# An attention and feed-forward layer: the attention result goes channel-major through DRAM instead of through transposes, orders are new, tiles are laid at multiples of 256 bytes

## What is computed

```python
def attn(x, w_qkv, b_qkv, w_out, b_out):          # 16 heads of 16 channels
    q, k, v = split(x @ w_qkv.T + b_qkv)
    scores = einsum('bhqd,bhkd->bhqk', q * hd ** -0.5, k) + mask
    out = einsum('bhqk,bhkd->bhqd', softmax(scores), v)
    return out.transpose(0, 2, 1, 3).reshape(B, L, D) @ w_out.T + b_out

def ffn(h, W1, b1, W2, b2):                       # 256 -> 1024 -> 256
    return relu(h @ W1 + b1) @ W2 + b2

x = x + layernorm(attn(layernorm(x), ...))
x = x + layernorm(ffn(layernorm(x), ...))
```

## Time and profile before

| | us |
|---|---|
| median of three runs (2044.54 to 2048.37) | 2048.34 |
| the profiled execution, its own time | 2041.29 |
| its span in the trace | 2039.5 |

### The profile page before, as it was taken

One profiled execution on the slowest core, in us unless ns is written; L12 is line 12 of the kernel. 1 busy time (PEld: TensorE's weight loads), 2 busy tenths in 40 slices (PEclk: granted clock), 3 DMA queues, 4 the chain that ended last, 5 costly groups with the idle time before them and its releaser, 6 DMA issues. The chain is left out here.

```text
span 2039.5 us, 71012 instructions
## 1 busy us (share of the span) xinstructions
PE 1926.4 (94%) x27904; PEld 1575.7 (77%) x27904; DVE 1511.4 (74%) x2913; ACT 1406.0 (69%) x2343; POOL 741.6 (36%) x910
## 2 busy tenths in 40 slices
PE   5789999999999999999999999999999999999985
PEld 3458888777878877888777788787788887778775
DVE  4687777787777778778777777777777777876731
ACT  1457767777776777776677777677777677776763
POOL 3113333334333334433343433333433333343343
PEclk7799999999999999999999999999999999999997
DMA  5333434433333433333343333343334344333200
GB/s 144 74 70 80 89 77 86 85 76 82 81 81 79 93 79 80 79 81 81 82 85 80 79 77 81 80 94 78 77 77 86 76 87 85 78 81 69 56 28 17
DMA packets 132815, 160.60 MB, mean 79 GB/s; under 512 B 29408, under 2 KB 82400, under 8 KB 132576
## 3 DMA queue, kind: packets, MB, share of 16 engines
q1 hardware_dynamic: 130544, 154.13, 35.7%
q10 hardware_dynamic: 2032, 2.69, 0.4%
HBM read 38.21 MB, written 17.83 MB: 27 GB/s over the span
## 5 line engine op out<-in xcount | busy, mean ns | idle before, releaser
L817 DVE TENSOR_REDUCE max_bias<-p_pair 128x4 f32<-128x1024 f32 (+1 forms) x640 | 772.8, 1222 | 262.0 <-PE p_pair L571 139.8
L742 ACT ACTIVATE probs<-p_pair 128x1024 f32<-128x1024 f32 x640 | 634.8, 1026 | 208.4 <-PE p_pair L568 127.6
L964 POOL TENSOR_TENSOR h_lo<-h_f,h_hi 128x512 fp32r<-128x512 f32 x256 | 329.7, 1288 | 507.5 <-ACT h_hi L774 507.5
L571 PE MATMUL p_pair<-stack 49*128 49x256 f32 (+1 forms) x3072 | 319.6, 306 | 39.5 <-DVE max_bias L817 22.7
L774 ACT ACTIVATE h_f<-p_pair,b_s 128x256 f32<-128x256 f32 x512 | 248.8, 486 | 133.1 <-PE p_pair L598 133.1
L571 PEld LDWEIGHTS p_pair<-stack 49*128 49x128 f32 (+1 forms) x3072 | 226.9, 188 | 126.7 <-DVE max_bias L817 59.8
L598 PE MATMUL p_pair<-w_hi,h_hi 64*128 64x256 f32 x2048 | 309.4, 279 | 5.0 <-ACT h_hi L774 2.5
L598 PE MATMUL p_pair<-x_hi,w_hi 64*128 64x256 f32 (+1 forms) x2560 | 302.1, 306 | 9.6 <-DVE x_lo L827 5.2
L598 PE MATMUL p_pair<-w_hi,h_lo 64*128 64x256 f32 x2048 | 305.7, 275 | 0.0
L598 PE MATMUL p_pair<-w_lo,h_hi 64*128 64x256 f32 x2048 | 305.5, 275 | 0.0
L598 PE MATMUL p_pair<-x_hi,w_lo 64*128 64x256 f32 (+1 forms) x2560 | 297.7, 302 | 0.0
(11 more groups left out here) (81 smaller groups left out, 2792.9 us busy)
## 6 DMA issues: line engine op xcount, KB each, us to landing
stack<-qk SPq DMA_DIRECT2D x1536, 64.0 KB, 2.3
xr<-x SPq DMA_DIRECT2D x32, 512.0 KB, 4.2
out<-yf SPq DMA_DIRECT2D x64, 256.0 KB, 2.2
xa<-x SPq DMA_DIRECT2D x31, 512.0 KB, 3.8
shift_rows<-max_t SPq DMA_DIRECT2D x128, 8.0 KB, 1.4
stack<-shift_rows SPq DMA_DIRECT2D x128, 8.0 KB
probs<-w_qkv_t SPq DMA_DIRECT2D x2, 384.0 KB, 5.5
ya<-w ACTq DMA_DIRECT2D x1, 512.0 KB, 8.2
```

The lines of the kernel that those rows point to most:

```text
L571: last = nc.tensor.matmul(dst[:, j, col:col + HALF].rearrange("p (a n) -> p a n", a=2), stack[r, stationary, at, kb * P:(kb + 1) * P], two ...
L742: nc.scalar.activation(probs[:, prob_slot(quad, c), :, :], banks("scores", n)[:, :, :], ACT.Exp, scale=SCALE).then_inc(exp_done, 1)
L817: nc.vector.tensor_reduce(dst, src, axis=AX.X, op=ALU.max, negate=True).then_inc(red_done, 1)
L964: nc.gpsimd.tensor_tensor(h_parts[1][:, m:m + 2, :], h_f[:, n % 2, :, :], h_parts[0][:, m:m + 2, :].bitcast(F32), ALU.subtract).then_inc(h ...
```

## The change

The four `o_t` and the one `o2` of PE are gone, and with them five fills of a PSUM pair a batch. In their place the result stays channel-major and goes through DRAM:

- `store_o` (SP, 4 a batch) sends the 128x512 result of one `pv` to `o_rows` (256 KB), and its four rows of sums to `den_q` in SBUF (8 KB), spread over the partitions.
- `inverse` (DVE, 2 a batch) takes the reciprocals of 128x32 sums, `store_inv` sends them to `inv_rows` in DRAM, and `load_inv` brings them back, each row to 16 partitions (`inv_b`, 256 KB written a time).
- `load_o` (SP, 2 a batch) brings the 16 channels of 8 heads into `o_ch`, which is the memory of `ya` (256 KB); `normal_o` (DVE, 2 a batch) multiplies `o_ch` by `inv_b`; `o2_hi` and `o2_lo` split it in two halves of 128x512 each, SBUF to SBUF.
- Channels now come in the order channel of the head, then head; the rows of w_out are put in that order on the host side of the inputs. `o_t` has two buffers.

All five engines have new lists. The small and odd tiles stand behind the large ones, and `max_bias` is padded, so that every matmul operand begins at a multiple of 256 bytes from `w_hi`, but the slices of `values`.

```diff
 ORDER = {
     "PE": [
-        ("scores_max", 16, -2, 2), ("qk", 1, -1, 3), ("scores", 6, -2, 0), ("pv", 0, -2, 1),
+        ("f1", 7, -4, 3), ("qk", 2, -1, 1), ("scores_max", 1, -1, 0), ("max_t", 3, -2, 2), ("qk", 3, -1, 1),
...
-        bqk_s, b1_s = sb("bqk_s", [P, 4]), sb("b1_s", [P, KF])
         b2_s = sb("b2_s", [P, D])
-        minus_half, eps = sb("minus_half", [P, KB]), sb("eps", [P, KB])
         xa = sb("xa", [P, KB, D])
...
-        max_bias = sb("max_bias", [P, 2, 4 * KB + D])
-        o_t = sb("o_t", [P, L])
-        den = sb("den", [P, 2, 2 * KB])
-        o_n = sb("o_n", [P, KB, D])
+        o_t = sb("o_t", [P, 2, L])
+        inv_b = sb("inv_b", [P, KD, L])
+        o_rows = nc.dram_tensor("o_rows", [KD, H // 2, 32, L], F32, kind="Internal").ap()
+        inv_rows = nc.dram_tensor("inv_rows", [KD, H // 2, L], F32, kind="Internal").ap()
         ya = sb("ya", [P, KB, D])
+        o_ch = ya[:, :, :].rearrange("p (c a) n -> p c (a n)", c=KD)
...
+        max_bias = sb("max_bias", [P, 2, 5 * P // 2])
+        den_q, inv_q = sb("den_q", [P, KD, 2, DT]), sb("inv_q", [P, KD, 2, DT])
...
+                elif what == "store_o":
+                    wait(sp, ot_done, b, QUADS, n + 1)
+                    reached(sp, o_in[n // 2], rows_free)
+                    reached(sp, inv_done, den_free)
+                    sp.dma_start(den_q[:, n // 2, n % 2, :],
+                                 o_t[HD:P:32, n % 2, :].rearrange("h (m t) -> h m t", t=DT)).then_inc(den_in[n % 2], 16)
+                    sp.dma_start(o_rows[n // 2, heads].rearrange("h c n -> (h c) n"),
+                                 o_t[:, n % 2, :]).then_inc(o_out[n % 2], 16)
+                elif what == "load_o":
+                    wait(sp, o_out[0], b, 32, 16 * (n + 1))
+                    reached(sp, o_out[1], other)
+                    reached(sp, x1_done, added)
+                    sp.dma_start(o_ch[:, n, :], o_rows[n, :, 0:HD, :].rearrange("h c n -> c h n")).then_inc(o_in[n], 16)
+                elif what == "store_inv":
+                    wait(sp, inv_done, b, KD, n + 1)
+                    sp.dma_start(inv_rows[n].rearrange("(j h) (m t) -> (h m) j t", j=2, t=DT),
+                                 inv_q[:, n, :, :]).then_inc(inv_out[n], 16)
+                elif what == "load_inv":
+                    wait(sp, inv_out[n], b, 16, 16)
+                    reached(sp, on_done, read)
+                    sp.dma_start(inv_b[:, n, :],
+                                 inv_rows[n].unsqueeze(0).broadcast_to([HD, H // 2, L])).then_inc(inv_in[n], 16)
...
-                elif what == "o2":
-                    wait(pe, ev["o_t"], b, QUADS, QUADS)
-                    last = transposed(dst, lambda r, m: o_n[r, m % KB, m // KB * P:(m // KB + 1) * P], KD * KB)
-                elif what == "o_t":
-                    wait(pe, ot_done, b, QUADS, n + 1)
-                    last = transposed(dst, lambda r, m: o_t[r, m * P:(m + 1) * P], KB)
...
-                        wait(pe, ev["o2"], b, 1, 1)
+                        wait(pe, ev["o2"], b, KD, KD)
...
-                    wait(act, mm["o_t"], b, QUADS, n)
-                    nc.scalar.activation(o_t[:, :], banks("pv", n)[:, 0, :], ACT.Copy).then_inc(ot_done, 1)
+                    for s in (den_in, o_out):
+                        wait(act, s[n % 2], b, 32, 16 * (n // 2))
+                    nc.scalar.activation(o_t[:, n % 2, :], banks("pv", n)[:, 0, :], ACT.Copy).then_inc(ot_done, 1)
+                elif what == "o2_hi":
+                    wait(act, on_done, b, KD, n + 1)
+                    wait(act, mm["op"], b, 1, 0)
+                    nc.scalar.activation(o2_t[0][:, n, :], o_ch[:, n, :], ACT.Copy).then_inc(hi_done["o2"], 1)
...
+                elif what == "o2_lo":
+                    wait(dve, hi_done["o2"], b, KD, n + 1)
+                    nc.vector.tensor_tensor(o2_t[1][:, n, :], o_ch[:, n, :], o2_t[0][:, n, :].bitcast(F32),
+                                            ALU.subtract).then_inc(ev["o2"], 1)
...
+                elif what == "inverse":
+                    for j in range(2):
+                        wait(dve, den_in[j], b, 32, 16 * (n + 1))
+                    nc.vector.reciprocal(inv_q[:, n, :, :], den_q[:, n, :, :]).then_inc(inv_done, 1)
                 elif what == "normal_o":
-                    wait(dve, mm["o_t"], b, QUADS, n + 1)
-                    nc.vector.reciprocal(den[:, :, :], sums[:, :, :, HD]).then_inc(den_done, 1)
...
+                    wait(dve, inv_in[n], b, 16, 16)
+                    wait(dve, o_in[n], b, 16, 16)
+                    nc.vector.tensor_tensor(o_ch[:, n, :], o_ch[:, n, :], inv_b[:, n, :], ALU.mult).then_inc(on_done, 1)
```

## The result

The changed kernel took 2072.65 us in the median (2068.05 to 2074.81) beside 2048.36 us of the kernel before: 24 us more. The ratio over all runs of both is 1.0113, with a 95% interval of 1.009 to 1.0136. The changed kernel was not run again there, so steps measured against it are uncertain by 2 to 3 us. Forecast was 1995 us, and the range ended at 2043.

The account below looks back on a forecast made before the run. PE's work was taken to bound the kernel. Transposes -45, waits before scores jobs -10, fewer fillers +10, operands -13 and the end +5 gave -53 us, from 2048 to 1995 us; range for 8 in 10: 1950 to 2043.

Parts of the forecast that it names:

- What bounds the kernel: Steady batch: PE, busy 58.68 of 60.0 us at full clock, sets the batch; DVE and ACT have room.
- The transposes, -45: PE: four `o_t` and one `o2` go, 1.41 us a batch, 45 us in 32 batches, all gained.
- Rival B: PSUM pairs of banks set the pace, not PE's work; transposes were fillers, operands gain nothing: 2033 us, chance 0.14.
- Fewer fillers, +10: PE: some transposes stood in gaps and were no loss, so 10 us of the 45 is given back, between 0 and 35.
- Operands, -13: PE's `f1` matmuls: operands at multiples of 256 bytes win 0.40 us a batch, 13 us in all.
- The way through DRAM, 0: From last `pv` to `op`: the round trip takes 10.2 us, fits in about 14 us, and PE waits nothing.
- case A: The DRAM round trip is late, before `op` and DVE's maxima: 3.3 us a batch, 2100 us, chance 0.14.
- rival D: DVE's new products and POOL block each other in SBUF: 1.0 us a batch, 2027 us, chance 0.08.
- The end, +5: Last batch's chain: the way through DRAM has no cover there and adds 5 us, between 0 and 10.
- The sum: Whole kernel: the terms sum to -53 us, 2048 to 1995 us, about 58.2 us a batch in place of 60.0.

Follow-up runs that it names:

- the best kernel: Changed kernel with the doubled scores, `scores 4` ahead of `op 0`, `relu 1` ahead of `o2_hi 1`, and stationary operands 64 bytes above moving ones: 2023.46 us.
- the kernel with the doubled scores: Changed kernel with the matmuls of `scores_max` 8, 9, 10 and `scores` 18, 19 issued twice: 2056.56 us.
- the clock held: Changed kernel with the doubled scores, none of its 28 steady batches having a fall of the clock: 2056.56 us; without the DRAM path as well, 2005.2 us.
- all three repaired in part: Changed kernel with the doubled scores, two order swaps around the late `inv_b` (on PE and ACT), and operands 64 bytes apart: 2023.46 us.

## Why the prediction was wrong, step by step

**What bounds the kernel.** "So what PE has to do sets the batch" was read from 58.68 of 60 us busy. But that busy time is not work: without 1536 of its instructions PE was busy 10 us longer. Doubling the transposes cost 1.35 us a batch, cutting 38 of 48 gave 0.2 at best. It was level, not bound.

**The transposes, -45.** The failed step of the sum. The duration was right (1.41 us a batch, and +1.35 when doubled); that it would be *gained* was not. With 38 of 48 out, 0.2 us a batch came in the best batches, 7 us in all at most, and the falls that came with it took more than that. Rival B (the pairs set the pace) had that sign; its give-back of 35 us is near the 31 us that the cut kernel gives back of 38 (1.18 us a batch) in its best batches. I had held B down for "PE's idle time is 1.3 us of 60", a number that can't tell.

**Fewer fillers, +10.** The fillers' worth was not the gap that they filled but the clock. No term, and no rival, had TensorE's clock in it, though the earlier trace rows had a column for it. The price is some 1.7 us a fall in 17 more batches of 28, about 30 us; cut transposes with and without `o_t` 2 differ by 16 us for 11 batches' falls. The Trainium skill describes such a case, page "TensorE: Matmul & The Clock Gate", section "A second HAM failure mode: psum-queue depth-cycling": a kernel that cycles through PSUM banks idles between groups of matmuls often enough for the clock to fall and rise again and again. The traces agree in kind: the falls of the changed kernel come behind scores jobs with a wait of 0.2 to 0.4 us each, and in the kernel with cut transposes a change of 0.19 us in one such wait came with 11 more falls.

**Operands, -13.** Wrong in sign. The text had the alternative, "if the difference is rather that moving and stationary operand begin at different places", and put it at +16; measured is +19 with the layout alone, in which `f1` fell back too. The rule of the Trainium skill (page "SBUF — State Buffer", section "SBUF: two separate sides") that PE never waits on another reader of SBUF would have made the term 0. The 19 us come from where the two operands of PE's own matmuls begin, of which that rule says nothing.

**The way through DRAM, 0.** "I take the first, with 3 to 4 us of room" failed by the landing times. `load_inv` and `load_o` were put at the stack's 2.3 us and took 3.5 and 3.4; the inverse's store was put at the shift's 1.4 us and took 1.9. From the end of the second `inverse` to the second `normal_o` I had 4.6 us against 5.0 of room. Without the path DVE comes to the product after 5.5 us. In the batch from 586.68 it began after 5.7 us, in late ones after 7 to 8. And "DVE may wait 1 us without becoming the bound" was the wrong question: behind DVE's wait stood ACT's list and behind that PE's. The price was 1.6 us a batch, 51 us in all. That is half of what case A asked for (3.3 us), mainly by A's own mechanism. A also had the stack's loads late behind an SP that blocks in `load_inv`. SP does block there:

```profile
SPq L601 <- DMA inv_rows<-inv_q: 47.7, 31, 2.9
```

1.5 us a batch, but PE waited for the stack only 5 times in the whole run, 10.2 us in all (9 times, 9.0 us before).

**DVE and POOL** (rival D) meet, but only where the product is late already. In the best kernel's late batches the product of `normal_o` 1 falls beside POOL's `h_lo`:

```profile
635.00 1.52 DVE L927 TENSOR_TENSOR ya<-ya,inv_b 128x512 f32<-128x512 f32 x1 [1.46 <-DMA inv_b<-inv_rows]
```

```profile
634.67 1.30 POOL L1027 TENSOR_TENSOR h_lo<-h_f,h_hi 128x512 fp32r<-128x512 f32 x1 [11.75 <-ACT h_hi L841]
636.13 1.54 POOL L1027 TENSOR_TENSOR h_lo<-h_f,h_hi 128x512 fp32r<-128x512 f32 x1 [0.16 <-ACT h_hi L841]
```

1.52 us instead of the 0.69 that it takes alone, and POOL's next `h_lo` 1.54 instead of 1.29. In the changed kernel 19 of the 64 products met one, 1.05 us in the mean against 0.69: 7 us of DVE in all, and 12 us in the kernel with the doubled scores, where D had put 32. Without the path, where nothing is late, one product in 64 was lengthened. The exclusive lock that the Trainium skill states (page "SBUF — State Buffer", section "SBUF: two separate sides"), by which the later of the two waits until the first has ended, fits these lengths. In the 23 meetings of the kernel with the doubled scores in which the `h_lo` was first, the product ends 0.55 us after it.

**The end, +5.** +10.6, the right sign by luck and the wrong cause: without the path it is 144.5 us, the same but for 1.1. The layout alone makes 3.3; the order written for the end is what is left, and no run has it alone. The starts took 5.5 us more by the fourth `v_out` and no term had them. With the doubled scores that `v_out` comes at 216.1 us, as before the change, so the low clock is the likely cause.

**The sum.** Where the 53 us went: transposes gained about 7 instead of 45; the operands cost 19 instead of giving 13; the DRAM path cost some 50 instead of 0; the clock some 30. These can't be added up, since each hides the others: the path removed gives 49 us (with 8 falls fewer), the clock held 16, the layout back 8 to 11, and all three repaired in part give 49. What is left is a gain: the kernel without the path and with the clock held (2005.2 us) stands 60 us under the kernel before in the same layout (2065.1 us), where cutting the transposes in the old order brought some 7. So by difference the new order, together with the work that went from DVE, is worth some 50 us; the forecast had no such term. No run measures it by itself, and how it divides between the two stays open: the new order was not run with the old transposes.

## What to carry to other kernels

When PE shows 98% busy, double a job and cut it before you price its removal: work that shows in full when added may give nothing when taken away. Ask of each filler what waits it shortens, and read the granted clock batch by batch around it; here half-speed matmuls two jobs later were the price. For a wait on a DMA in an in-order list, count the jobs behind it on *every* engine that it reaches, and price the landing by DMAs of the same size and kind: here 256 KB took 3.5 us into SBUF and 64 KB took 2.4.

## What the runs showed of the hardware that was not expected

- The pace of matmul pairs with 256 columns (fp32r, 64 rows each) depends on where the two operands begin, modulo 256 bytes: 120 ns at distance 0, 118 to 119 at -64 and 128, 113 to 116 with the stationary operand 64 above. Four layouts agree in the order of these, in two kernels. The weights lay at a multiple of 256 in all of them. Why, the runs don't say.
- Adding 1.2 us of useless matmuls to a batch made the kernel 16 us faster, and removing 1.2 us of transposes made another 15 us slower, both through the granted clock in one job of 2.3 us.
- Transposes count for the clock here: eight in place of two ahead of `pv` 3 took the falls from 19 to 8 of 28 batches, in one profiled run of each.
- A DVE product with both inputs in SBUF that began while a `h_lo` of POOL ran ended 0.55 us after that `h_lo`, 23 times of 23 in the kernel with the doubled scores, and took up to 1.63 us instead of 0.69. That gave 20 of 28 batches one length, though `inv_b` landed up to 0.9 us apart in them.
